# A vision block on one core: four edits to queues, PSUM banks and ScalarE's order

## What is computed

```python
h = einsum('bnd,ed->bne', patches(x), W)                 # 64 images, 49 patches of 768, to 192
# layer 1: 12 heads of 16, causal, a learned position term in the keys
qkv = h @ w_attn + b_attn
probs = softmax(causal(q * 0.25 @ k.T + q * 0.25 @ rel.T))
h = layernorm(h + (probs @ v) @ w_proj + b_proj)
# layer 2: a router picks 2 of 8 experts for every token
probs8 = softmax(h @ Wg.T + bg); combine = top-2 of probs8, zeros elsewhere
delta = (einsum('td,erd->ter', h, A) + ba) * combine[:, :, None]
qkv = h @ Wqkv.T + bqkv + 2 * (einsum('ter,eor->to', delta, Bm) + combine @ bb)
h = layernorm(h + attention(qkv) @ Wproj.T + bproj)
```

## Time and profile before

| | us |
|---|---|
| median of three runs | 447.51 |
| the profiled execution | 446.53, its span 444.7 |
| TensorE matmuls busy | 398.6 (90% of the span) |
| VectorE busy | 295.0 (66%) |
| ScalarE busy | 231.7 (52%) |
| GpSimd busy | 116.6 (26%) |
| mean granted TensorE clock | 0.958 of full speed |
| slots 2, 3 and 4 on TensorE | 40.65 to 47.12 to 54.35 to 62.49, that is 6.5, 7.2 and 8.1 |
| first use of `lora` (L540) and of `w2` (L484) | at 61.83 and at 72.36 |

### The profile page before, as it was taken

One profiled execution on the slowest core, in us unless ns is written; L12 is line 12 of the kernel. 1 busy time (PEld: TensorE's weight loads), 2 busy tenths in 40 slices (PEclk: granted clock), 3 DMA queues, 4 the chain that ended last, 5 costly groups with the idle time before them and its releaser, 6 DMA issues.

```text
span 444.7 us, 13552 instructions
## 1 busy us (share of the span) xinstructions
PE 398.6 (90%) x5270; PEld 348.5 (78%) x5270; DVE 295.0 (66%) x783; ACT 231.7 (52%) x727; POOL 116.6 (26%) x237
## 2 busy tenths in 40 slices
PE   5874997999989999999999999989998999887974
PEld 4763886878878898889888899778886988776853
DVE  7051566857677676876687767696578758777572
ACT  1341455465565656555665555646655565544442
POOL 1110112230233213432242222333223223313122
PEclk9995999999999999999999999999999999996875
DMA  8452221210212111220221212111101110111010
GB/s 282 131 159 63 50 80 18 51 38 15 48 28 62 50 48 28 64 54 11 50 64 25 57 45 58 28 19 30 18 19 19 30 18 19 17 23 22 14 32 23
DMA packets 49353, 21.23 MB, mean 48 GB/s; under 512 B 41278, under 2 KB 45601, under 8 KB 49226
## 3 DMA queue, kind: packets, MB, share of 16 engines
q1 hardware_dynamic: 48714, 19.64, 18.1%
q10 hardware_dynamic: 576, 0.73, 0.5%
HBM read 13.13 MB, written 2.41 MB: 35 GB/s over the span
## 4 chain that ended last, share of the span: by engine, by line
PE 73%; ACT 9%; DVE 8%; issue 5%; DMA 3%; SPq 1%; POOLq 0%; POOL 0%; ACTq 0%; DVEq 0%
PE ps L414 11%; PE ps L484 10%; PE ps L497 8%; PE ps L472 7%; PE ps L519 5%; PE ps L508 5%; PE ps L449 4%; PE ps L453 4%; PE ps L451 4%; PE ps L436 3%; PE ps L438 3%; PE ps L520 3%; DVE mx L763 2%; PE ps L540 2%; ACT q L646 2%
## 5 line engine op out<-in xcount | busy, mean ns | idle before, releaser
L763 DVE TENSOR_REDUCE mx<-ps 113x12 f32<-113x588 f32 x64 | 49.2, 769 | 75.4 <-PE ps L472 74.8
L378 POOL TENSOR_SCALAR kbd<-k,const 64x294 f32<-64x294 f32 x128 | 69.1, 549 | 98.1 <-ACT q L646 88.0
L667 ACT COPY pt<-ps 113x339 f32<-113x339 f32 x128 | 50.7, 445 | 52.1 <-PE ps L497 51.7
L385 POOL TENSOR_SCALAR shift<-mv,rstd 128x1 f32<-128x1 f32 (+1 forms) x50 | 13.2, 264 | 216.4 <-ACT rstd L702 216.4
L414 PE MATMUL ps<-tokw,xs 128*128 128x192 f32 (+1 forms) x300 | 57.1, 342 | 9.1 <-DVE res L791 4.8
L775 DVE TENSOR_REDUCE psum<-probs 113x12 f32<-113x588 f32 x64 | 48.4, 756 | 23.7 <-ACT probs L653 22.9
L414 PEld LDWEIGHTS ps<-tokw,xs 128*128 128x128 f32 (+1 forms) x300 | 50.7, 197 | 11.4 <-DVE res L791 6.4
L497 PE MATMUL ps<-const,probs 113*113 113x113 f32 x384 | 52.1, 274 | 3.4 <-DVE probs L784 2.6
L784 DVE TENSOR_TENSOR probs<-probs,rsum 113x588 f32<-113x588 f32 x64 | 51.4, 802 | 2.2
L497 PEld LDWEIGHTS ps<-const,probs 113*113 113x113 f32 x384 | 47.2, 186 | 6.6 <-issue 5.1
L770 DVE TENSOR_TENSOR probs<-ps,mx 113x588 f32<-113x588 f32 x64 | 49.4, 772 | 2.2
(11 more groups left out here) (79 smaller groups left out, 704.2 us busy)
## 6 DMA issues: line engine op xcount, KB each, us to landing
xs<-in_x SPq DMA_DIRECT2D x24, 384.0 KB, 3.7
vbd<-vrow SPq DMA_DIRECT2D x160, 18.4 KB
out<-o SPq DMA_DIRECT2D x24, 96.0 KB, 1.7
tail<-in_pos SPq DMA_DIRECT2D x1, 656.0 KB, 16.2
tokw<-in_tokw ACTq DMA_DIRECT2D x3, 192.0 KB, 3.4
w<-in_w SPq DMA_DIRECT2D x1, 472.5 KB, 10.0
xs<-in_x SPq DMA_DIRECT2D x3, 128.0 KB, 3.2
p<-in_p SPq DMA_DIRECT2D x2, 145.5 KB
```

What stands on the lines that cost most here:

```text
L378: last = nc.gpsimd.tensor_scalar(L.kbd[t % 2][:, e], L.k[:, :, at:at + T], kmask[:, e:e + 1], 1.0, ALU.mult, ALU.mult)
L667: nc.scalar.copy(pt[n % 2][:, 3 * half:3 * half + 3, :].rearrange("p g i -> p (g i)"), ps[0:PP, 2 + half, 0:3 * PP]).then_inc(pt_ready[hal ...
L763: nc.vector.tensor_reduce(mx[:].rearrange("p (b h) -> p b h", b=2), score_view, AX.X, ALU.max).then_inc(mx_ready, 1)
```

## The change

Four edits:

- **Queues.** The pixel loads `x[1]` to `x[4]` and the first third of the position rows are issued on ScalarE's queue at the start, and each refill on ScalarE's queue right after the copy `h` of the block it replaces.
- **Late weights.** `lora`, `w2`, `b2`, the last part of the position rows and `p2` are issued by the sync engine in slots 1, 2, 3, 4 and 6, behind the values placed in those slots. The position rows are cut in three instead of two.
- **Bank.** `transpose_hw` writes bank 3 instead of bank 7. `route` waits until VectorE has made the previous `hw` instead of until ScalarE has copied `hwt`; the next `transpose_probs`, which writes bank 3 too, waits for that copy.
- **Order.** In ScalarE's slot the logarithms (`inverse_deviation`, both layers) come behind the first layer's `vrow`, `k` and `q` instead of in front of them.

```diff
@@ sync
-            load_x(1)
             sp.dma_start(w1a[:], w1a_in).then_inc(w1a_loaded, 16)
             sp.dma_start(w1b[:], w1b_in).then_inc(w1b_loaded, 16)
-            sp.dma_start(tail[64:128, 0:POS], pos_in[:, 0:POS]).then_inc(pos_loaded[0], 16)
-            load_x(2)
-            load_x(3)
+            sp.dma_start(tail[64:128, POS:2 * POS], pos_in[:, POS:2 * POS]).then_inc(pos_loaded[1], 16)
             sp.dma_start(p1[:], p1_in).then_inc(p1_loaded, 16)
-            sp.dma_start(tail[64:128, POS:TOK], pos_in[:, POS:TOK]).then_inc(pos_loaded[1], 16)
-            sp.dma_start(lora[:], lora_in).then_inc(lora_loaded, 16)
-            load_x(4)
-            sp.dma_start(w2[:], w2_in).then_inc(w2_loaded, 16)
-            sp.dma_start(b2[:], b2_in).then_inc(b2_loaded, 16)
-            sp.dma_start(p2[:], p2_in).then_inc(p2_loaded, 16)
+            def load_late(n):
+                if n == 1:
+                    sp.dma_start(lora[:], lora_in).then_inc(lora_loaded, 16)
+                if n == 2:
+                    sp.dma_start(w2[:], w2_in).then_inc(w2_loaded, 16)
+                if n == 3:
+                    sp.dma_start(b2[:], b2_in).then_inc(b2_loaded, 16)
+                if n == 4:
+                    sp.dma_start(tail[64:128, 2 * POS:TOK], pos_in[:, 2 * POS:TOK]).then_inc(pos_loaded[2], 16)
+                if n == 6:
+                    sp.dma_start(p2[:], p2_in).then_inc(p2_loaded, 16)
...
             for n in range(FIRST, SLOTS):
-                for b in embeds(n):
-                    if b + XS < BLOCKS:
-                        sp.wait_ge(emb_done, b + 1)
-                        load_x(b + XS)
                 for t in tiles_from(n - 1, QKV1):
                     place_values(L1, t, SLOT1)
                 for t in tiles_from(n - 1, QKV2):
                     place_values(L2, t, SLOT2)
+                load_late(n)
@@ tensor
-            def transpose_probs(n):
+            def transpose_probs(n, free):
                 if n > 0:
                     pe.wait_ge(yt_ready, n)
+                if free:
+                    pe.wait_ge(*free)
                 pe.wait_ge(p_ready, n + 1)
@@ route
-                    pe.wait_ge(hwt_ready, b)
+                    pe.wait_ge(hw_ready, b)
@@ transpose_hw
-                nc.tensor.transpose(ps[0:1 + NE, 7, 128:128 + k], comb[0:k], ident[0:k, 0:k])
-                nc.tensor.transpose(ps[0:ER, 7, 0:k], hw[0:k], ident[0:k, 0:k]).then_inc(hwtr_done, 1)
+                nc.tensor.transpose(ps[0:1 + NE, 3, 128:128 + k], comb[0:k], ident[0:k, 0:k])
+                nc.tensor.transpose(ps[0:ER, 3, 0:k], hw[0:k], ident[0:k, 0:k]).then_inc(hwtr_done, 1)
+                return hwt_ready, b + 1
...
@@ scalar
             act.dma_start(const[:], const_in).then_inc(const_loaded, 16)
+            act.dma_start(tail[64:128, 0:POS], pos_in[:, 0:POS]).then_inc(pos_loaded[0], 16)
+            def load_x(b):
+                act.dma_start(xs[:, b % XS], x[b]).then_inc(x_loaded[b % XS], 16)
+            for b in range(1, XS):
+                load_x(b)
             def take_h(b):
                 act.wait_ge(emb_done, b + 1)
                 nc.scalar.copy(h[0:k, b, :], ps[0:k, 5, 0:E]).then_inc(h_ready, 1)
+                if b + XS < BLOCKS:
+                    load_x(b + XS)
...
                 for b in qkv2s(n):
                     take_v(L2, b, SLOT2)
                     take_qk(L2, b, SLOT2)
+                for b in turns(n):
+                    take_v(L1, b, SLOT1)
+                    take_qk(L1, b, SLOT1)
                 for b in out1(n):
                     inverse_deviation(L1, b)
                 for b in out2(n):
                     inverse_deviation(L2, b)
-                for b in turns(n):
-                    take_v(L1, b, SLOT1)
-                    take_qk(L1, b, SLOT1)
                 for b in embeds(n):
                     take_h(b)
```

More of the change, by code:

```diff
@@ L291, in build @@
         w1b_loaded = sem("w1b_loaded")
-        pos_loaded = [sem(f"pos_loaded{u}") for u in range(2)]
+        pos_loaded = [sem(f"pos_loaded{u}") for u in range(3)]
         p1_loaded = sem("p1_loaded")
@@ L307, in _ @@
         def _(sp):
-            def load_x(b):
-                sp.dma_start(xs[:, b % XS], x[b]).then_inc(x_loaded[b % XS], 16)
             for u in range(3):
                 sp.dma_start(xs[:, 0, 2 * u:2 * u + 2], x[0, :, 2 * u:2 * u + 2]).then_inc(x0_loaded[u], 16)
-            load_x(1)
             sp.dma_start(w1a[:], w1a_in).then_inc(w1a_loaded, 16)
             sp.dma_start(w1b[:], w1b_in).then_inc(w1b_loaded, 16)
-            sp.dma_start(tail[64:128, 0:POS], pos_in[:, 0:POS]).then_inc(pos_loaded[0], 16)
-            load_x(2)
-            load_x(3)
+            sp.dma_start(tail[64:128, POS:2 * POS], pos_in[:, POS:2 * POS]).then_inc(pos_loaded[1], 16)
             sp.dma_start(p1[:], p1_in).then_inc(p1_loaded, 16)
-            sp.dma_start(tail[64:128, POS:TOK], pos_in[:, POS:TOK]).then_inc(pos_loaded[1], 16)
-            sp.dma_start(lora[:], lora_in).then_inc(lora_loaded, 16)
-            load_x(4)
-            sp.dma_start(w2[:], w2_in).then_inc(w2_loaded, 16)
-            sp.dma_start(b2[:], b2_in).then_inc(b2_loaded, 16)
-            sp.dma_start(p2[:], p2_in).then_inc(p2_loaded, 16)
+            def load_late(n):
[9 more added lines that the diff above has]
+                    sp.dma_start(p2[:], p2_in).then_inc(p2_loaded, 16)
             def place_values(L, t, slot_of):
@@ L557, in values2 @@
                         (hwt[:, b % HB2], b2[:])]
+            bank3 = None
             bank4 = None
@@ L583, in _ @@
                         pe.wait_ge(zeros_ready, 2)
-                    transpose_probs(n - 1)
+                    transpose_probs(n - 1, bank3)
                 for b in turns1(n):
@@ L599, in _ @@
                         pe.wait_ge(pos_loaded[0], 16)
-                    if first_token(b) + tokens(b) > POS >= first_token(b):
+                    if first_token(b) == POS:
                         pe.wait_ge(pos_loaded[1], 16)
+                    if first_token(b) == 2 * POS:
+                        pe.wait_ge(pos_loaded[2], 16)
                     bank6 = project_v(L1, b, values1(b), bank6)
@@ L610, in _ @@
                 for b in routers(n):
-                    transpose_hw(b)
+                    bank3 = transpose_hw(b)
                 for b in turns1(n):
@@ L692, in take_hw @@
                 act.wait_ge(hwtr_done, b + 1)
-                nc.scalar.copy(h1t[C:C + 1 + NE, 0, b % HB2, 0:k], ps[0:1 + NE, 7, 128:128 + k])
-                nc.scalar.copy(hwt[:, b % HB2, 0:k], ps[0:ER, 7, 0:k]).then_inc(hwt_ready, 1)
+                nc.scalar.copy(h1t[C:C + 1 + NE, 0, b % HB2, 0:k], ps[0:1 + NE, 3, 128:128 + k])
+                nc.scalar.copy(hwt[:, b % HB2, 0:k], ps[0:ER, 3, 0:k]).then_inc(hwt_ready, 1)
             def inverse_deviation(L, b):
```

## The result

The changed kernel took 428.46 us, the median of four runs (426.79 to 435.3), against 449.51 for four runs of the kernel before (447.36 to 452.06): a ratio of 0.9517, with a 95% interval from 0.9427 to 0.9608. The 435.3 counts as a slow run, which the ratio leaves out; the other three have a median of 427.37. As ratios to 447.51 the forecast was 0.966 and its lower bound 0.959. The profiled execution took 426.79, its span 425.0 against 444.7: 19.7 us less, where the sum had 15.2.

A forecast was written before the change was run, and what follows sets the result against it. TensorE, working 90% of the span, was held mainly by a 9.6 us wait for late-issued values. Terms summed to -15.2 from a profiled 446.53, 431.4; plus 0.98 for a median, 432.3 us, range 429 to 439.

The forecast's parts named there:

- the sum: All gains and costs of the queue, bank and order edits added up: -15.2 us for the whole kernel.
- its lower bound: The fastest time allowed, with all gains and no costs: 429.4 us, given as 429 in the range.
- The wait and the slow slot: TensorE's wait for the first values goes, -9.56 us, and the low clock in the slot after it, -2.84.
- The first position rows: Moved to ScalarE's queue, they shorten TensorE's 0.9 us wait at the first product by 0.3, at most 0.4.
- Nothing in the queue came late afterwards: Sync queue after the first values: value DMAs and late weights still land in time, cost 0.
- the 8.28: The longest DMA issue on the sync queue, 8.28 us, said to come behind `p1`.
- The estimate of 5 us for `p1`: `p1` on one DMA engine takes some 5 us before the first values; the stall-stays rival, chance 0.06.
- an order that is late, not bandwidth: First value rows: they come late through issue order, as the DMA engines are a quarter busy meanwhile.
- The refills on ScalarE: Twenty later pixel loads behind copies `h` cost 0, at most 8.6 us; exposed-loads rival, chance 0.09.
- Taken as a forecast for the whole edit: If landing were bandwidth-bound, the queue edits would be worth nothing and the sum about -2.5 us.
- The router's bank: Route no longer waits for ScalarE's last copy in five slots: -4.82 us, less 0.5 for new waits.
- The logarithms: Moved behind `q`, they lengthen TensorE's wait for `yt` in five slots, +2.15 us, and shorten one, -0.3.

The follow-up runs named there:

- `loads_only`: Kernel before with pixel loads moved to ScalarE's queue, the weights still issued early, bank and order as before: 447.37 us.
- `late_only`: Kernel before with late weights behind the first values, pixel loads kept on the sync queue, bank and order as before: 438.36 us.
- `queues_only`: Kernel before with the queue edits (pixel loads on ScalarE's queue, late weights), bank 7 and ScalarE's old order kept: 437.88 us, ratio 0.9724.
- `order_only`: Kernel before with only ScalarE's order changed, logarithms behind the first layer's copies: 450.66 us, ratio 1.0062.
- both repeats: The changed kernel run again twice, unchanged, one execution each: 431.92 and 431.68 us.
- `filled`: Changed kernel with logarithms between `vrow` and `k`, plus 18 unread matmuls in TensorE's gaps from slot 57 on: 422.51 us, ratio 0.9435.
- `filled_start`: `filled` plus six more unread matmuls in TensorE's gaps of the first 22 us: 422.52 us, ratio 0.9401.
- `mid_order`: Changed kernel with the logarithms between `vrow` and `k`: 430.79 us, ratio 0.9578.
- `p1_on_act`: Changed kernel with `p1` and `lora` issued on ScalarE's queue in front of `x[1]` to `x[4]`: 438.3 us.

## Why the prediction was right, and where it was wrong

**The wait and the slow slot** (forecast 9.56 + 2.84 + 0.3): 12.40 by slot 2, against 12.7. The first position rows brought nothing: the wait only changed its last arrival, to `w1b`. Nothing in the queue came late afterwards, as argued. Of the argument one part was wrong: I named the pixel loads as what stood in front of the values, counted two long issues where the trace has three, and put the 8.28 behind `p1` where it is behind `lora`. `loads_only` and `late_only` show that it was `lora`, `w2`, `b2`, `p2` and the last position rows, by the long issues directly behind `p1`, `lora` and `p2`. The prediction cites the Trainium skill for one DMA engine at a transfer over 97 partitions ("DMA: Bandwidth & Descriptors", "Why a DMA increments its semaphore by 16 and not by 1"). The trace agrees: `p1`, `lora` and `p2`, all of 97 partitions, have a single late landing each where `w1b` has sixteen. The estimate of 5 us for `p1` was too short: `p2`, of the same size, took 8.6 us even when issued apart from the others. So "an order that is late, not bandwidth" holds for the mean share of 0.24, not for the work that lay one behind the other in these three; no run here changed the 97 partitions.

**The refills on ScalarE** (forecast 0, bound 8.6): at most 0.05 from slot 3 to 59 in `queues_only`. What the Trainium skill says on spreading DMAs over the issuing engines ("DMA: Bandwidth & Descriptors", "Rules for kernel authors") agrees with `loads_only`, where the move by itself brought nothing. Taken as a forecast for the whole edit it would have been wrong, since the edit also changed the order in the sync queue.

**The router's bank** (forecast 4.82 less 0.5): 5.09 in the first four slots and 0.95 at slot 60, less 0.29: 5.75. This is a mis-sized term, 1.4 us too small: the four waits gave 0.9 more than their rows say, the fifth, 0.62 by its row, 0.3 more, and the new wait of the transposes came in just the three tightest slots, at 0.10 each, which is 0.2 less than the 0.5.

**The logarithms** (forecast +2.15 and -0.3): +1.81 and -0.31. Slot 22 took 0.13 and not 0.43: TensorE's wait for `yt` grew there by 0.42 too, but the embedding's product, which started 0.42 us after the transposes L530 before, started 0.22 us after them now; it had been held up by something else anyway. The sign was right, and `order_only` shows it by itself.

**The end** is the step that failed. Neither the sum nor its bounds have a term for it: the sum treated the last 40 us as a copy of the trace of before, its low clock phases with it, and its lower bound of 429 left no room for a shorter one. In the execution measured the phase at slot 60 was short, worth 2.7 us, and the last one began later, 0.5. Together with the 1.4 of the bank, and less the small terms, that is the difference between 15.2 and 19.7. The error of 1.4 in the bank alone would have left the time inside the range. By the long phase of both repeats the edits are worth 15.68 + 0.95 = 16.6 us, and 447.51 less 16.6 is 430.9, inside the range. The six executions of the changed kernel have a median of 430.6, the five without the 435.3 one of 429.5. Four of the six lie inside the range and two below it, so luck has a part in the miss, as it would have had in a hit. The kernel before varies as much: its four runs span 447.36 to 452.06. What decides from one execution to the next whether the phase is short or long stays open; the edits don't need to be part of it, since the same program showed both. `filled` shows what can be done about it: without idle time there, the phase goes.

The best version is `filled` (`filled_start` is as good): all of the queue and bank edits, the logarithms between `vrow` and `k`, and the fillers, 0.9435 of before.

## What to carry to other kernels

Read a queue from the late transfer backwards, but do not blame the instruction with the long issue: blame what stands in front of it, and test by moving that alone. Put a step that is not urgent into a gap that the engine has anyway; moved behind the urgent copies, it can land in front of the next urgent one, and costs its full length where the reader already waits. Where the time depends on a stretch that the last trace shows at the lower clock, give that stretch a term and a bound of its own, and run the same program again before an edit gets the credit. Compare two traces by where one recurring instruction ends, slot by slot: steps of 0.1 us show, and what belongs to the clock separates from what belongs to the edit.

## What the runs showed of the hardware

- One program had executions of 425.0 and 430.1 us of span, another 444.7 and 450.2, with equal slots to 0.02 us elsewhere. All of the difference was in stretches at the lower clock level and in the arrival of the first data.
- The lower level came during or after waits of TensorE (the 9.56 us wait, the waits near slots 58 to 60, the end). Near 72 and 297 us (3.15 and 1.68 us lost) it came with waits of 1.49 and 0.91 us, after which the other execution of the same program kept the upper level.
- Adding 8.4 us of useless matmuls into gaps at the end shortened the kernel by 6.7 us of span against `mid_order` (426.0 to 419.3); 1.7 of it is that kernel's phase near 115 us.
- A DMA issue on ScalarE's queue started 0.01 us after the start of the copy in front of it and did not delay the next one. In `p1_on_act` four issues held ScalarE for 7.75 us when two transfers of 97 partitions stood in front.
- Three transfers of 97 partitions (145.5, 103.1 and 145.5 KB) issued within 15 us landed 14.0, 16.6 and 16.1 us after their issue, at 19.41, 26.82 and 36.08; issued late, `lora` took 6.8 and `p2` 8.6 us. The DMA issued directly behind each took 4.32, 8.28 and 8.06 us in the first case, 0.83 and 0.80 in the second.
